# Where the projections' store queue carries the first two groups of self-attention loads

## The reference

```
x = x + attn(layernorm(x))
# attn: q = x Wq + bq (16 heads of 16), k = x Wk + bk, v = x Wv + bv (4 key heads of 16),
#       softmax(q k^T / 4) v for the 4 query heads of each key head, then Wo, bo
x = x + cross_attention(layernorm(x), ctx, mask)
x = x + experts(layernorm_scale_bias(x))
```

## Time and profile before

| | us |
|---|---|
| median of 3 runs (1892.76 to 1900.6) | 1895.57 |
| the profiled execution | 1891.45 |
| its span | 1889.7 |
| TensorE busy in the span | 1787.9 (95%) |
| VectorE, ScalarE busy | 1266.1 (67%), 1036.9 (55%) |
| last matmul of the projections ends | 86.12 |
| first matmul of the attention starts | 100.13 |

### The profile page before, as it was taken

One profiled execution on the slowest core, in us unless ns is written; L12 is line 12 of the kernel. 1 busy time (PEld: TensorE's weight loads), 2 busy tenths in 40 slices (PEclk: granted clock), 3 DMA queues, 4 the chain that ended last, 5 costly groups with the idle time before them and its releaser, 6 DMA issues. The chain is left out here.

```text
span 1889.7 us, 36142 instructions
## 1 busy us (share of the span) xinstructions
PE 1787.9 (95%) x12036; PEld 1187.4 (63%) x12037; DVE 1266.1 (67%) x2510; ACT 1036.9 (55%) x2238; POOL 363.0 (19%) x403
## 2 busy tenths in 40 slices
PE   6889999999999999988989999997899999999998
PEld 3443333333333333366978899996698888888887
DVE  6588999999999999133248899994757322222323
ACT  2305878888887888921228888885226333333332
POOL 3000000000000000040004222221030444555440
PEclk9956999999999999988899999998999999999999
DMA  5601122111112210045210212111615233333333
GB/s 181 185 10 27 29 39 39 31 28 28 28 28 39 39 30 3 3 119 161 93 54 16 87 32 85 32 31 62 215 58 163 50 50 50 50 50 51 52 56 126
DMA packets 95151, 118.63 MB, mean 63 GB/s; under 512 B 18844, under 2 KB 76624, under 8 KB 93968
## 3 DMA queue, kind: packets, MB, share of 16 engines
q1 hardware_dynamic: 80016, 97.56, 18.7%
q0 software_dynamic: 13920, 19.15, 6.4%
q10 hardware_dynamic: 1104, 0.43, 0.1%
HBM read 70.37 MB, written 41.48 MB: 59 GB/s over the span
## 5 line engine op out<-in xcount | busy, mean ns | idle before, releaser
L497 DVE TENSOR_REDUCE half_max<-psA 128x1 f32<-128x512 f32 x1024 | 634.3, 684 | 36.8 <-PE psA L547 36.4
L528 ACT ACTIVATE PT<-psB 128x1024 f32<-128x1024 f32 x512 | 517.6, 1025 | 164.7 <-PE psB L557 164.5
L547 PE MATMUL psA<-KS,QS 48*128 48x512 f32 x1024 | 407.1, 481 | 23.4 <-PEq L102 14.0
L557 PE MATMUL psB<-QS,KS 50*128 50x512 f32 x1024 | 364.0, 458 | 0.4 <-ACT PT L528 0.4
L576 PE MATMUL psO<-PT,VG 128*32 128x256 f32 x4096 | 329.3, 394 | 4.7 <-ACT OU L518 0.8
L547 PEld LDWEIGHTS psA<-KS,QS 48*128 48x128 f32 x1024 | 168.9, 195 | 247.6 <-DVE half_max L497 188.9
L1866 DVE TENSOR_TENSOR m_silu<-m_psU,m_silu 128x512 f32<-128x512 f32 x104 | 71.8, 691 | 216.4 <-PE m_psU L1694 216.4
L576 PEld LDWEIGHTS psO<-PT,VG 128*32 128x32 f32 x4096 | 82.2, 108 | 191.0 <-issue 120.8
L1347 ACT ACTIVATE x_probs<-x_scores,x_neg_max 128x77 f32<-128x77 f32 x512 | 176.3, 358 | 2.9 <-DVE x_neg_max L1253 2.8
L557 PEld LDWEIGHTS psB<-QS,KS 50*128 50x128 f32 x1024 | 145.1, 187 | 19.9 <-ACT PT L528 17.4
L1197 PE MATMUL psYx<-VO,x_ET 128*128 (+1 forms) x640 | 146.0, 383 | 1.4 <-ACT x_ET L1370 0.9
(11 more groups left out here) (208 smaller groups left out, 2737.7 us busy)
## 6 DMA issues: line engine op xcount, KB each, us to landing
QS<-q_parts SPq DMA_DIRECT2D x96, 128.0 KB
q_parts<-part SPq DMA_DIRECT2D x16, 512.0 KB, 2.7
OT<-OU SPq DMA_DIRECT2D x32, 256.0 KB, 2.6
KS<-k_parts SPq DMA_DIRECT2D x32, 128.0 KB
xf_rows<-XF SPq DMA_DIRECT2D x32, 128.0 KB, 1.7
acc<-X SPq DMA_DIRECT2D x32, 128.0 KB, 1.8
m_x<-xf_rows SPq DMA_DIRECT2D x32, 128.0 KB, 2.1
WG<-in_Wg SPq DMA_DIRECT2D x8, 512.0 KB, 4.1
```

Of the source, the lines that this page charges most:

```text
L497: dve.tensor_reduce(half_max[:, h * TB + t, n:n + 1], psA[:, bank_of(slot, 2 * v + r), :], axis=AX.X, op=ALU.max).then_inc(max_taken, 1)
L528: act.activation(PT[:, k % 4, 2 * a:2 * a + 2, :].rearrange("p h n -> p (h n)"), psB[:, u % 2, :, :].rearrange("p a n -> p (a n)"), ACT.Ex ...
L547: pe.matmul(psA[:, bank_of(slot, m), :], QS[top:top + KQ, slot, h // 2, t * P:(t + 1) * P], KS[top:top + KQ, slot, n * HALF:(n + 1) * HALF ...
L557: mm = pe.matmul(psB[:, u % 2, r, :], KS[top:top + KM, slot, c * P:(c + 1) * P], QS[top:top + KM, slot, a, half * HALF:(half + 1) * HALF], ...
```

## The change

SyncE's block of the projections is written as a plain loop over the eight quads. Each quad's three stores come as before. The load of group 0 stands behind the stores of quad 3 and that of group 1 behind the stores of quad 5 (`GROUP_AT`), where before they stood in front of the stores of quads 6 and 7. The wait on `stored` in front of a load is gone; ScalarE's waits make sure that quads 0 and 1 are in HBM before quad 3's pieces exist, and quads 2 and 3 before quad 5's. The wait on `consts` stands once, in front of group 0.

```diff
+        GROUP_AT = (3, 5)
...
-            def step(quad):
-                if t := quad(2):
-                    i, e = t
...
-                    if isinstance(i, int) and i >= NQ - 2:
-                        sp.wait_ge(stored[e], NSTORE * (NQ // 2 - 2))
-                        sp.wait_ge(consts, 7)
-                        load_group(sp, T, i - (NQ - 2), e)
-                    for m, rows in MS:
-                        sp.wait_ge(low_done, at(i, NM, m + 1))
...
-            staggered(sp, NQ, range(3), step)
+            for i in range(NQ):
...
+                for m, rows in MS:
+                    sp.wait_ge(low_done, i * NM + m + 1)
...
+                    sp.dma_start(to.rearrange("j r n -> r j n"), part.bitcast(F32)[0:rows, e, :, m, :]).then_inc(stored[e], 16)
+                if i in GROUP_AT:
+                    if i == GROUP_AT[0]:
+                        sp.wait_ge(consts, 7)
+                    load_group(sp, T, GROUP_AT.index(i), GROUP_AT.index(i) % SLOTS)
```

More of the change, by code:

```diff
@@ L157, in _ @@
                     sp.wait_ge(x_loaded[n], 16)
-            def step(quad):
-                if t := quad(2):
-                    i, e = t
-                    b = i // (S // HALF)
-                    tokens = bass.ds(i % (S // HALF) * HALF, HALF)
-                    if isinstance(i, int) and i >= NQ - 2:
-                        sp.wait_ge(stored[e], NSTORE * (NQ // 2 - 2))
-                        sp.wait_ge(consts, 7)
-                        load_group(sp, T, i - (NQ - 2), e)
-                    for m, rows in MS:
-                        sp.wait_ge(low_done, at(i, NM, m + 1))
[L173 to L177, removed]
-            staggered(sp, NQ, range(3), step)
+            for i in range(NQ):
+                e, b = i % 2, i // (S // HALF)
+                tokens = slice(i % (S // HALF) * HALF, (i % (S // HALF) + 1) * HALF)
+                for m, rows in MS:
+                    sp.wait_ge(low_done, i * NM + m + 1)
+                    if m < 2:
+                        to = q_parts.rearrange("b j g h d n -> b j (g h d) n")[b, :, m * P:(m + 1) * P, tokens]
+                    else:
+                        to = k_parts.rearrange("b j g d n -> b j (g d) n")[b, :, :, tokens]
+                    sp.dma_start(to.rearrange("j r n -> r j n"), part.bitcast(F32)[0:rows, e, :, m, :]).then_inc(stored[e], 16)
+                if i in GROUP_AT:
+                    if i == GROUP_AT[0]:
+                        sp.wait_ge(consts, 7)
+                    load_group(sp, T, GROUP_AT.index(i), GROUP_AT.index(i) % SLOTS)
             for e in range(2):
```

## The result

The changed kernel took 1887.64 us (median of 8 runs, 1880.18 to 1893.59) against 1898.2 us for the kernel before (8 runs, 1890.52 to 1903.02): ratio 0.9948, 95% interval 0.9924 to 0.9973, a gain of some 10 us with 5 to 14 in the interval. On a second chip, 12 runs against 26, it was 1886.34 against 1894.1 us, ratio 0.9963 (0.9946 to 0.998), 7 us. The two profiled executions are 1880.94 us (the change, 6.7 under its median) and 1891.45 us (before).

What follows compares the result with a forecast made beforehand. TensorE's 14.01 us gap after the projections, waiting for a store queued behind L86's two engines, was taken as the bound; landing at 90.0 instead of 99.6 gains 9.6: 1895.57 - 9.6 = 1886.0 us, range 1878.5 to 1892.5.

Steps and rivals of the forecast that it cites:

- What bounds the stretch: End of projections: TensorE idle 14.0 us, 9.5 of it slow landing of the last store behind L86's two engines.
- The prices on the two engines: DMA queue in the projections: 11.8 us for a group's load, 3.2 us for a quad's stores.
- strict turn: Two engines' queue served without overlap: two groups and four quads from 53.8 us, last store landed at 91.7 us.
- The choice of 90.0 within 88.9 to 91.7: Last store's landing at the projections' end: 90.0 us taken against 99.6 before, a gain of 9.6 us.
- the mix of before: Loads and stores mixed as in the kernel before, whose trace was 3.0 us better than strict turn.
- the rival of the engines that fall behind: Projections' DMA queue: strict turn plus 1.4 us held-up issue, landing at 93.1 us; gain 6.5, median 1889.1 us; 18%.
- The cover of ScalarE's copy: Quad 6's first copy at 73.22 us waits for quad 4's stores, landed by 71: some 2 us spare, no cost.
- Nothing removed, nothing added elsewhere: SyncE's dropped and moved waits and straight code change nothing; the later scores, paced by VectorE, keep the 9.6 us.
- The rival of the clock: Scores and first group: shorter gap keeps the clock up, 5.7 us more; gain 15.3, median 1880.3 us; 15%.
- The signs: Profile after: SyncE's wait 3 to 5 us, gap 4.4, scores at 90.5, 0.13 at about 61 to 66 and 79 to 84.
- Slower by the buffer: ScalarE's quad 6 copy into `part`: quad 4's stores land 14.8 us late, time 1901 us; 3%.
- no effect at all: Last store's 12.5 us landing is its own; end of block only 99.6 to 98.4 us, median 1894.4; 4%.

Runs made afterwards that it cites:

- split_before: Kernel before with k's high part copied by two loads of 16 rows instead of one twofold broadcast load; TensorE's gap 10.4 us against 14.0.
- split_after: Changed kernel with k's high part copied by two loads of 16 rows instead of the broadcast; median 1882.35 us, ratio 0.9938 to the kernel before.
- fill: Changed kernel with an added 192-column matmul behind each of the last 44 scores ahead of the first group; 1907.76 us.
- g0_alone: Kernel before with only group 0's load moved, behind quad 3's stores, group 1's still between quads 6 and 7; TensorE's gap 11.3 us against 14.0.
- g1_alone: Kernel before with both groups' loads behind quad 5's stores, so only group 1's load moved ahead; TensorE's gap 17.8 us against 14.0.

## Why the prediction was right, and where it was not

The time was forecast as 1886.0 us and came to 1887.64, a gain of 9.6 forecast and some 10.6 (7.8 on the second chip) between medians. Both the forecast 9.6 and the 7.2 us of gap lie within the interval of 5 to 14. By its steps:

- **What bounds the stretch: right in the main.** The gap at the end of the block, the wait for the last store behind it, and two engines of sixteen that carry L86: taking the broadcast away removed the stretch at 0.13 and 3.6 us of the gap, with nothing moved. But the prediction gave the two engines all of the 9.5 us of slow landing, and `split_before` leaves them 3.4; the rest is a load on all engines in front of the store. After the change the two engines are nearly the whole excess (`split_after`: 3.3 us to land instead of 6.7). The last store holds both parts of its 64 rows of k, not the low half; nothing hangs on that.
- **The prices on the two engines: their sum right to a microsecond, the terms less so.** In strict turn the last store was to land at 91.7 us; it landed at 92.1, with the projections 0.3 us earlier. The price of a quad, 3.2 us, is the distance of the last two landings. From the first load's issue at 53.3 to quad 4's landing were 18.2 us against 16.5 reckoned, from quad 5's landing to quad 6's 13.5 against 15.0; the two errors nearly cancel.
- **The choice of 90.0 within 88.9 to 91.7: wrong.** This is the step that failed: "I take 90.0, in the lower half". The reason given was the mix of before, 3.0 us better than strict turn "since the other fourteen engines go on to stores while two are at L86"; but stores on the other fourteen take nothing off the two, and after the change no such saving shows. Perhaps two groups and two quads overlapped before because they stood close together, while now each group has two quads behind it; no run shows this. The gap shrank by 7.2 us, not 9.6; the truth lay with the rival of the engines that fall behind, between its 6.5 and the strict turn's 7.9, without the hold-up of SyncE's issue that this rival added (0.62 us for the last store, not 2.07).
- **The cover of ScalarE's copy: right, and thinner than said.** Quad 4's last store landed at 71.5 us instead of 71, the copy ran at 72.9 without waiting: 1.4 us of cover, not 2. With the loads one quad earlier, a wait appeared at quad 7's copy (3.4 us, nearly all of it in place of one for TensorE).
- **Nothing removed, nothing added elsewhere: right.** No wait of SyncE for `consts`; the scores keep VectorE's pace (busy 37.08 us from 92.62 to 130.5).
- **The rival of the clock: its mechanism was not borne out, its price was.** The clock fell in every profile, with gaps from 17.8 us down to 1.1. But the forecast took the 46.9 us of the first group for a constant, and it ranges from 42.8 to 51.8 where nothing is added among the scores. In the profile it gave 2.6 us on top of the gap, which is how a gap of 7.2 us came out near the forecast 9.6: the total was nearer than its main term, by chance. The forecast also started from 1895.57 us; the eight runs put the kernel before at 1898.2.
- **The signs: mixed.** SyncE's wait is 6.1 us (3 to 5 forecast), the first scores start at 92.6 us (90.5), and 0.13 shows at 66 us but not at 79 to 84. A two-engine tail behind 91 us, named as a sign of being wrong, is there as the end of the stretch from 90 us; the clock of 0.50 at the first group's start is as forecast.

Slower by the buffer, and no effect at all, were rivals that the rows above rule out.

## What to carry to other kernels

Here a load whose outer dimension is a copy count of 2 ran on two of sixteen engines, and a store issued behind it on the same queue waited for those engines; the store's landing time then told its place in their queue, and a stretch at a small, constant DMA share (0.13) told how many they were. Before moving such a load, add up what stands ahead of the last store on the busiest engine, in strict turn, and take a better case only with a reason that reaches that engine. Or give the load an outer dimension that spreads: that halved the gap here as well as an earlier place did, but the later groups took 1.5 us longer with it. When single runs differ by more than the term in question, compare the term itself in the profiles, here the idle time before one matmul.

## What the runs showed that I had not expected

- The clock needs long to rise in the first group, and differs from run to run: 9 to 31 us after the group's matmuls begin in the twelve profiles without added matmuls among the scores; a unit (one exp and its matmuls) of the group takes 2.15 us at the low clock and 13.2 / 11 = 1.20 in the row from 157.8 us above, so a microsecond of low clock costs 0.44, and by this estimate some 20 us more of it make 52 out of 43.
- A TensorE that was busy for all of 33 us with alternating 48-row and 128-row matmuls stayed at 1.2 GHz (`fill`).
- SyncE can be held at the issue itself: two stores that took 0.94 us to issue in `g0_alone` took 6.72 in `g1_alone`.
- Sixteen busy engines move 403 GB/s at stores, but 142 GB/s at a group's load. That the load writes 16 rows at a time may be the reason; it was not tried.
